# One context bank instead of two, three general banks in a ring, and new written-out orders for all engines of a cross-attention kernel

## The reference

```
qn = layer_norm(q, q_norm_g, q_norm_b);  kvn = layer_norm(kv, kv_norm_g, kv_norm_b)
Q, K, V = heads(qn @ Wq), heads(kvn @ Wk), heads(kvn @ Wv)
attn = softmax(einsum('bhqd,bhkd->bhqk', Q, K) / sqrt(32))
ctx = einsum('bhqk,bhkd->bhqd', attn, V)
out = q + gelu(ctx @ Wo + bo, approximate=False)
```

## Time and profile before

| what | value |
| --- | --- |
| median of 3 runs | 3454.32 us |
| the profiled execution, its time | 3452.61 us |
| its span, first to last instruction | 3450.8 us |
| TensorE clock granted, mean | 0.995 |
| PE busy | 3348.2 us, 97% |
| DVE, ACT, POOL busy | 2265.5, 2335.3, 2311.7 us: 66%, 68%, 67% |
| one batch in the middle, by the starts of its matmuls | 105.46 us |

### The profile page before, as it was taken

One profiled execution on the slowest core, in us unless ns is written; L12 is line 12 of the kernel. 1 busy time (PEld: TensorE's weight loads), 2 busy tenths in 40 slices (PEclk: granted clock), 3 DMA queues, 4 the chain that ended last, 5 costly groups with the idle time before them and its releaser, 6 DMA issues.

```text
span 3450.8 us, 60367 instructions
## 1 busy us (share of the span) xinstructions
PE 3348.2 (97%) x16611; PEld 2141.9 (62%) x16611; DVE 2265.5 (66%) x4775; ACT 2335.3 (68%) x3986; POOL 2311.7 (67%) x1543
## 2 busy tenths in 40 slices
PE   7999999999999999999999999999999999999998
PEld 5566666666666666666666666666666666666664
DVE  6666666676676666666766766666667667666664
ACT  4576666766666766667666667666676666676665
POOL 1767666767667676677676676766776766767665
PEclk9999999999999999999999999999999999999999
DMA  5556566556556565665565565656655655656553
GB/s 131 78 103 101 97 107 106 82 103 103 105 94 95 102 101 97 107 106 82 102 103 105 94 95 102 101 97 107 107 82 101 104 105 94 95 102 101 96 83 68
DMA packets 186492, 340.15 MB, mean 99 GB/s; under 512 B 20561, under 2 KB 20577, under 8 KB 186466
## 3 DMA queue, kind: packets, MB, share of 16 engines
q1 hardware_dynamic: 186000, 339.03, 58.0%
q10 hardware_dynamic: 466, 0.80, 0.2%
HBM read 104.87 MB, written 33.55 MB: 40 GB/s over the span
## 4 chain that ended last, share of the span: by engine, by line
PE 79%; DVE 10%; issue 6%; ACT 5%; DMA 0%; DVEq 0%; POOL 0%; ACTq 0%
PE gen L788 36%; PE score L807 14%; PE score L814 12%; PE ctx L833 11%; DVE maxes L654 6%; PE gen L845 4%; ACT probs L517 2%; PE gen L879 1%; ACT xT L542 1%; DVE ctx_n L665 1%; DVE cT L635 1%; PE gen L899 1%; DVE gen L695 1%; ACT act_out L534 1%; ACT cT L542 1%
## 5 line engine op out<-in xcount | busy, mean ns | idle before, releaser
L436 POOL TENSOR_TENSOR probs<-probs 128x1024 f32<-128x1024 f32 x762 | 1803.8, 2398 | 342.7 <-PE ctx L833 338.3
L654 DVE TENSOR_REDUCE maxes<-score 128x1 f32<-128x512 f32 x2048 | 1313.4, 681 | 210.5 <-PE score L814 197.1
L517 ACT ACTIVATE probs<-score 128x512 f32<-128x512 f32 x2048 | 1122.0, 604 | 223.5 <-PE score L807 195.5
L814 PE MATMUL score<-k_stack,q_stack 96*128 96x512 f32 x2048 | 746.8, 427 | 5.9 <-DMA q_stack<-q_nat 3.8
L807 PE MATMUL score<-q_stack,k_stack 128*128 128x512 f32 x2048 | 734.7, 420 | 11.2 <-ACT q_stack L569 5.8
L451 POOL TENSOR_TENSOR rstd<-var_eps,minus_half 128x1 f32<-128x1 f32 x256 | 141.6, 553 | 639.1 <-DVE neg_mean L685 638.8
L807 PEld LDWEIGHTS score<-q_stack,k_stack 128*128 128x128 f32 x2048 | 375.8, 188 | 254.1 <-ACT probs L517 118.7
L814 PEld LDWEIGHTS score<-k_stack,q_stack 96*128 96x128 f32 x2048 | 376.0, 188 | 246.4 <-ACT probs L517 72.9
L833 PE MATMUL ctx<-probs,v_sb 128*32 128x512 f32 x4096 | 480.5, 598 | 0.0
L788 PE MATMUL gen<-w_v,cT 128*128 128x512 f32 x1536 | 413.7, 394 | 0.6 <-issue 0.6
L788 PE MATMUL gen<-xT,w_q 128*128 128x512 f32 x1536 | 396.9, 394 | 6.7 <-ACT v_sb L528 6.6
(11 more groups left out here) (92 smaller groups left out, 2801.6 us busy)
## 6 DMA issues: line engine op xcount, KB each, us to landing
k_stack<-k_nat SPq DMA_DIRECT2D x384, 256.0 KB, 6.7
q_stack<-q_nat SPq DMA_DIRECT2D x381, 256.0 KB, 6.8
tok<-in_x SPq DMA_DIRECT2D x132, 256.0 KB, 10.4
tok<-in_ctx SPq DMA_DIRECT2D x128, 256.0 KB, 10.8
res<-in_x SPq DMA_DIRECT2D x124, 256.0 KB, 2.8
out<-res SPq DMA_DIRECT2D x124, 256.0 KB, 2.9
probs<-in_L_xattn_Wq SPq DMA_DIRECT2D x1, 1024.0 KB, 8.5
probs<-in_L_xattn_Wk SPq DMA_DIRECT2D x1, 1024.0 KB, 10.7
```

What stands on the lines that cost most here:

```text
L436: pool.tensor_tensor(probs[:, c + 1, heads], probs[:, c + 1, heads], probs[:, c, heads], ALU.add).then_inc(pool_added, 1)
L517: act.activation(probs[:, n, part, :], score_at(s, "st", i)[:], ACT.Exp, scale=SCALE).then_inc(exp_done, 1)
L654: dve.tensor_reduce(maxes[:, u1 % 2, SROW + i:SROW + i + 1], score_at(s, "s", i)[:], AX_X, ALU.max, negate=True).then_inc(max_done, 1)
L814: pe.matmul(score_bank(pe, b, s, "s", i)[:, :], q_stack[0:KROWS, u1 % 2, n, P * part:P * (part + 1)], k_stack[0:KROWS, u1 % 2, n, :], star ...
```

## The change

The context bank becomes one, and the general banks three, taken in turn by position in the list of a batch (`bank_before` gives the tile that had the bank last, across the batch boundary too). The wait of the first `pv` half of unit t is now for `cn` of unit t - 1. The orders of all five engines are written anew: the same items, 200 of TensorE's for each batch in both versions, in other places. In the list of TensorE the two halves of `pv` now stand apart in all four steps (before: in steps 1 and 3), and `z` stands apart from `pv` in all (before: in all but step 3). At the end of the last batch and in the preparation some products use other banks.

```diff
...
 
 
 PARTS = 3
+NGEN = 3
+NSCORE = 4
 OVER_BATCH = ("v", "o", "gelu", "res_add", "store", "res", "load", "ln", "la", "lv", "norm", "x", "first_res", "ob")
 ORDER = {
     "pe": (
-        "q*3 z st*4 v*2 st*2 s v s*2 st*2 v s st*2 s v s st s*2 v st s st s st s st s st s*4 pv*2 m k*3 o*3",
-        "st*2 q st*2 q st q st k*2 st*2 k x st*2 s st pv s*3 z st x s st*2 s x st x st s*3 x pv x*2 s*4 x o*4 s o "
-        "s*2 o m o*2",
-        "o k st*2 k s*2 k st*2 s st z st*2 s st s st s st s st s st s st s st*2 s st s*5 pv*2 m q*3",
-        "k*2 st*3 k q st*2 q st*3 q st*4 pv z s st*4 s*2 v s pv s*4 v s*2 v s*3 v s*2 v s v m",
+        "q*2 v q st*4 v st s v s st s st v st*2 s*2 z st v st s st v s*3 st pv s st s*2 k st s st s*3 pv m o k*2 "
+        "o",
+        "st*3 o st*3 q*3 st z st x st x st k st k*2 s st s x st x st*3 pv x s*2 x s*2 pv s*2 x s*2 o*2 s o x s*4 "
+        "o*2 s o*2 m",
+        "o*2 k*2 s st s st k st z st s st s st s st*2 s st*2 s*2 st s st q st*4 pv s*4 q s*2 q s pv m",
+        "k q v k st*4 k st*2 q st*4 q st z st*4 v st s*3 pv s*4 v s*3 v s*2 v s*3 v s pv m",
     ),
     "act": (
-        "q st*6 split st*2 v st*3 norm st*5 v mh mx*3 k mx norm*2",
-        "st*2 gelu st*2 q st*4 x norm st k st norm st norm st x st*2 x st*2 x norm x norm x*3 gelu*2 mh mx*4 "
-        "split",
-        "gelu st*2 k st*14 split mh mx*3 q mx",
-        "st*8 k st*4 q st*4 v split v mh mx*4",
+        "q st*12 v norm split norm v st*4 norm mh mx*4 k",
+        "st*6 gelu q st x*2 st*3 norm st norm st x k norm x st*4 x norm x norm x gelu x mh gelu mx*4 split",
+        "gelu st k st*11 split st*4 q mh mx*4",
+        "st*6 k st*5 q st*5 v split v mh mx*4",
     ),
     "dve": (
-        "q zt zr zb cn ln s ln s*2 ln la*2 s lv s la s*3 lv s*4 ln la s lv s*2 lv s md ml k ln",
-        "ln ob la ln q la lv ln s lv x la lv k la s*3 zt s x lv s x s*2 zr x*2 s zb x*2 s cn x s*2 ob s*4 ob md "
-        "ml ob",
-        "s*2 k s zt s zr s*9 zb s*2 cn s md ml q",
-        "k s q zt zr s*2 zb cn s*13 md ml",
+        "q s ln s*2 ln*2 la s*2 la lv zt la zr lv zb s cn lv s*10 md ml ln k",
+        "ob ln*2 la*2 ln la lv ln q lv zt zr la x*2 lv zb la cn s lv s x lv k x s*2 x s x s*3 x s*3 ob s*4 x s md "
+        "ob ml",
+        "ob s*2 zt s*2 zr s zb s*4 cn k s*7 md q ml",
+        "k zt zr zb cn q s*16 md ml",
     ),
     "pool": (
-        "ln*2 split ln add*5 res_add ln*2 add",
-        "ln*3 add*4 res_add*2 add split add",
-        "res_add add*6 split",
-        "add*5 split add",
+        "ln*3 split add*6",
+        "ln*2 res_add ln*2 add ln add*3 res_add add res_add add split",
+        "split add*6",
+        "res_add add split add*5",
     ),
     "sp": (
-        "load*7 rq load rk store res",
-        "rk rq store res store*2",
-        "first_res rk rq",
+        "load*8 rq rk",
+        "store res rq rk store res store",
+        "rk first_res rq store",
         "first_res rq rk",
     ),
 }
...
             _off = _s + {"q": 2, "k": 2, "m": 1, "z": -1}[_kind]
             GEN_AT[(_kind, _off % NU)] = len(GEN)
             GEN.append((_kind, _off // NU, _off % NU, NU))
-assert len(GEN) % 2 == 0
+
+
+def bank_before(i, count, banks):
+
+    batch, at = divmod(i, count)
+    return i - banks if at >= banks else batch * count - 1 - (count - 1 - at) % banks
 
 
 def build(nc, x, ctx_in, q_g, q_b, kv_g, kv_b, wq, wk, wv, wo, bo, out):
...
-        score = [ps(f"score{i}") for i in range(NC)]
-        ctx_ps = [ps(f"ctx{i}") for i in range(2)]
-        gen = [ps(f"gen{i}") for i in range(2)]
+        score = [ps(f"score{i}") for i in range(NSCORE)]
+        ctx_ps = ps("ctx")
+        gen = [ps(f"gen{i}") for i in range(NGEN)]

...
-                return (ctx_ps[NU % 2], gen[1 - GEN_AT[("z", NU - 1)] % 2])[n]
+                return gen[(GEN_AT[("z", NU - 1)] + 1 + n) % NGEN]

...
             return b + (s + off) // NU, (s + off) % NU
 
         def gen_at(kind, n):
-            return gen[GEN_AT[(kind, n)] % 2]
+            return gen[GEN_AT[(kind, n)] % NGEN]
 
         def gen_bank(eng, b, kind, n):
 
-            back = GEN_AT[(kind, n)] - 2
+            back = bank_before(GEN_AT[(kind, n)], len(GEN), NGEN)
             while back > -3 * len(GEN):
                 kind2, off, n2, per = GEN[back % len(GEN)]
                 b2 = b + off + back // len(GEN)
                 if valid(b2):
                     wait(eng, free[kind2], b2 * per + n2 + 1)
                     break
-                back -= 2
+                back = bank_before(back, len(GEN), NGEN)
             return gen_at(kind, n)
 
         def score_at(s, kind, i):
-            return score[SCORE_AT[(s, kind, i)] % NC]
+            return score[(PER_STEP * s + SCORE_AT[(s, kind, i)]) % NSCORE]
 
         def score_bank(eng, b, s, kind, i):
-            back = PER_STEP * s + SCORE_AT[(s, kind, i)] - NC
+            back = bank_before(PER_STEP * s + SCORE_AT[(s, kind, i)], PER_STEP * NU, NSCORE)
             while back > -2 * PER_STEP * NU:
                 b2, s2 = b + back // (PER_STEP * NU), back % (PER_STEP * NU) // PER_STEP
                 kind2, i2 = SCORES[s2][back % PER_STEP]
...
                         if kind == "cn" and valid(bp):
                             wait(dve, z_spread, tp + 1)
                             wait(dve, pv_done, 4 * tp + 4)
-                            dve.tensor_tensor(ctx_n[:], ctx_ps[up % 2][:], ctx_n[:], ALU.mult).then_inc(ctx_read, 1)
+                            dve.tensor_tensor(ctx_n[:], ctx_ps[:], ctx_n[:], ALU.mult).then_inc(ctx_read, 1)
                         if kind == "ln" and valid(b + 1):
                             wait(dve, tile_loaded[n], 16 * (b + 2))
                             dve.bn_stats(stats[:, n, :], tok[:, n, :]).then_inc(ln_stats, 1)
...
                             pe.matmul(score_bank(pe, b, s, "s", i)[:, :], q_stack[0:KROWS, u1 % 2, n, P * part:P * (part + 1)],
                                       k_stack[0:KROWS, u1 % 2, n, :], start=True, stop=True).then_inc(s_full, 1)
                         if (kind, n) == ("pv", 1) and last(b) and s == NU - 1:
-                            wait(pe, ctx_read, NU * B - 1)
                             wait(pe, ctx_split, NU * B - 2)
-                            last_products((0,), (0, 1))
                             for kind2, count in (("z", NU * B - 1), ("m", NU * B), ("q", NU * B), ("k", NU * B),
                                                  ("x", 2 * NC * B), ("v", NC * B), ("o", NC * (B - 1))):
                                 wait(pe, free[kind2], count)
-                            last_products((1,), (0, 1))
+                            last_products((0, 1), (0, 1))
                         if kind == "pv" and valid(b):
                             wait(pe, exp_done, 16 * t + 8 * n + 8)
                             if n == 0:
-                                wait(pe, ctx_read, t - 1)
+                                wait(pe, ctx_read, t)
                             if s == 0:
                                 wait(pe, free["v"], 4 * b + 2 * n + 2)
                             for c in (2 * n, 2 * n + 1):
                                 for j in range(HU):
                                     lo = P * s + DH * j
-                                    mm = pe.matmul(ctx_ps[s % 2][DH * j:DH * (j + 1), :], v_sb[:, c, lo:lo + DH],
+                                    mm = pe.matmul(ctx_ps[DH * j:DH * (j + 1), :], v_sb[:, c, lo:lo + DH],
                                                    probs[:, c, j, :], start=(c == 0), stop=(c == NC - 1))
                                     if n == AFTER_ST[s] and c % 2 == 0 and j == 0:
                                         mm.then_inc(stack_used, 1)
...
```

More of the change, by code:

```diff
@@ L314, in score_bank @@
                     break
-                back -= NC
+                back = bank_before(back, PER_STEP * NU, NSCORE)
             return score_at(s, kind, i)
@@ L617, in prepare @@
                     dve.wait_ge(bias_mm, 3)
-                    dve.tensor_copy(bias_v[:], ctx_ps[1][:, 0:NU]).then_inc(bias_cols, 1)
+                    dve.tensor_copy(bias_v[:], score[3][:, 0:NU]).then_inc(bias_cols, 1)
                     dve.wait_ge(bias_cols, 2)
@@ L627, in prepare @@
                     dve.wait_ge(bo_mm, 1)
-                    dve.tensor_copy(bias_all[:], ctx_ps[0][:]).then_inc(bo_ready, 1)
+                    dve.tensor_copy(bias_all[:], ctx_ps[:]).then_inc(bo_ready, 1)
                     low_weights(3, "o", None)
@@ L747, in prepare @@
                         for c in range(NC):
-                            mm = pe.matmul(ctx_ps[1][:, u:u + 1], probs[:, 2, c, P * u:P * (u + 1)],
+                            mm = pe.matmul(score[3][:, u:u + 1], probs[:, 2, c, P * u:P * (u + 1)],
                                            norm_cols[:, 3, c:c + 1], start=(c == 0), stop=(c == NC - 1))
@@ L762, in prepare @@
                     for u in range(NU):
```

(4 more changed lines are left out.)

## The result

The changed kernel takes 3350.9 us, the median of four runs (3350.2 to 3351.1), against 3455.1 us for the kernel before in the same series: ratio 0.9698, 95% interval 0.9682 to 0.9715. The forecast was 3376 us, faster, range 3335 to 3445. The gain is 104 us where 78 were forecast.

The account below looks back on a forecast made before the run. TensorE was taken to bound the kernel, by gaps between its starts. Per batch -1.8 (runs), -2.2 (m), +1.0 (blocks), +0.3 and +0.2 (new waits) gave -2.5 us; x 31 = -78 us, so 3376 us, range 3335 to 3445.

Parts of the forecast that it names:

- m: TensorE's waits around m in steps 1 and 3 mostly go, with more work ahead of m: -2.2 us per batch.
- Blocks: Separate groups of pv or z matmuls, twelve instead of nine, cost TensorE 0.33 us each: +1.0 us per batch.
- Runs: Scores fifth or later in an unbroken run wait for bank readers, 0.10 us each; 18 fewer: -1.8 us per batch.
- new waits: TensorE waits for cn with the single context bank, +0.3 us per batch, and for GpSimd's adds, +0.2.
- The sign for this term: Weight loads of scores waiting for exps were to fall by a third or more.
- What I had left unnamed before: Loss in a batch of the kernel before that the three named losses don't explain: 2.7 us in the prediction.
- The ends: Preparation and tail: a few tenths of a us once; the two end batches raise the count from 30 to 31.
- Rival A: Other waits, at VectorE's and ScalarE's pace, take most of the gain: -0.4 us per batch, 3442 us; chance 0.20.
- Rival B: Single context bank makes adds, z, cn and next pv a serial loop: +1.0 us per batch, 3485 us; chance 0.10.

Follow-up runs that it names:

- the edit of step 2: Changed kernel with step 2's first pv half moved beside the second, behind the step's last scores: 3549.6 us, ratio 1.0272 to the kernel before.

## Why the prediction was right, and where its sizes were off

The bound, TensorE's own starts and not its busy share, was right: a batch lost 3.1 us, the work on all engines stayed.

- *m*: forecast -2.2, measured 2.43 to 0.2. Right. The reason given for the 1.17 us of step 1 was ob alone; by the earlier trace rows ob was half of it, and the second third ahead of m did more than the move of ob.
- *Blocks*: forecast +1.0. Each lone pv half and z still costs 0.33 us in the trace after, twelve times; the edit of step 2 shows the same price. Right. The prediction's 0.44 us for an x has such a price in it too: the x itself takes 0.36 in the mean of the changed kernel, and the score behind it 0.09 more than its free pitch.
- *Runs*: forecast -1.8, and *new waits*, forecast +0.5, together -1.3. Measured is what the -3.1 of a batch leave without m and blocks: -3.1 + 2.2 - 1.0 = -1.9. The term that was mis-sized is the new waits. In the whole trace pv waits for cn once (1.1 us) and z for the adds once (0.8 us), where 0.3 and 0.2 in every batch were charged. The runs came out as forecast where they were counted: by the lateness of each score's start against the free pitches and the prices of blocks and x, the scores that stand fifth or later lose 3.2 us at 32 places before and 1.6 at 14 after, 0.10 and 0.11 each, so -1.7. But the first four scores of the runs, which had no term, lose 2.0 instead of 1.2, and what was lost in step 1 beside m is 1.2 less. What I had left unnamed before, 2.6 us, is 2.5 after. The sign for this term was badly chosen: the weight loads wait longer for exps while the counted scores lose less, so that wait doesn't measure what a run loses.
- *By place this came out otherwise.* The sums of the steps over free pitch (from the starts of matmuls, mean of 30 batches, us) and what blocks at 0.33, m, and scores at 0.10 explain of them:

| step | over, before | named | over, after | named |
| --- | --- | --- | --- | --- |
| 0 | 1.75 | 1.6 | 1.72 | 1.2 |
| 1 | 3.90 | 2.5 | 1.27 | 1.0 |
| 2 | 3.11 | 2.7 | 3.14 | 2.2 |
| 3 | 2.47 | 1.9 | 2.00 | 1.2 |

  Step 1 lost 1.2 us of unnamed waits (single scores 0.3 us late among the x); steps 0, 2 and 3 together got 1.1 that were not there, half of it step 2's late ScalarE. The right sum hides that two errors of that size cancelled. That step 2 would gain by its shorter run did not come true as long as ScalarE's read of k stood in it.
- *The ends*: a few tenths were forecast beside one more batch. The windows of the preparation are these, of the kernel before and of the changed one:

```profile
0.00:172.37 172.37, 146.82 (x656) 93.78 (x656) 106.60 (x244) 92.97 (x158) 79.71 (x76) 0.93 0.57 105
```
```profile
0.00:167.49 167.49, 146.32 (x657) 92.84 (x657) 106.55 (x244) 91.97 (x158) 72.70 (x73) 0.95 0.59 108
```

  4.9 us here and 3.7 at the tail (114.7 to 111.0) are 8.6, where x 31 had allowed 2.5. The granted clock is higher in the mean in both ends (0.93 to 0.95, 0.94 to 0.97): fewer us at half clock. As an estimate, if TensorE set the pace there, the lost clock is (1 - clock) x window: 12.1 and 6.9 us before, 8.4 and 3.3 after. So up to some 7 of the 8.6 us can be the clock, which the prediction had no term for; what of it is the order wasn't tried. 30 x 3.1 + 8.6 = 101.7 us is the difference of the two profiled spans. The medians differ by 104, since that of the kernel before lies 2.5 us above its profiled execution.

Rival A held in one place, step 2: there ScalarE's work inside the run paces TensorE until the read of k is out of it; then the pitch is the 0.33 of four banks. Rival B didn't come, neither as a wait for cn nor for the adds. But its loop is real: with a first half 4 us later it costs 3.2 us of wait, and in 22 of 30 batches the halved clock behind it.

What the orders alone, or the banks alone, are worth stays open: with two general banks the new order can't run, since TensorE would wait at z for a bank that ScalarE frees only behind exps of scores that stand after z; with one context bank the old order can't, since it has pv ahead of z in two steps. It wasn't tried with a third order.

## What to carry to other kernels

Read a saturated engine by the distances between its starts, count what it would take alone, and give each excess a place; here that gave the time within 1%, though not each place. Don't count banks or covers alone: an item inside a run of producer and consumer costs its full time if the consumer has to do it within the run, and nothing behind the run (14 us here for one word of an order moved). A written-out order that is balanced on several engines has local slacks of tenths of a us. Of the eight edits here that moved one or two items, five made it slower, two changed nothing and one made it faster; look what is queued behind the moved item, on the DMA queues too.

## What the runs showed of the hardware

- One pause of TensorE of 3.2 us in a stream of matmuls brought the granted clock from 1.00 to 0.50 in 22 of 30 batches, in 13 of them for some 6 us, so a wait of 3.2 us cost 3.0 to 5.5 us, 4.5 in the mean. A pause of 1.6 us, with shorter waits behind it, did so in 5 of 30. The mean clock of the first kernel is 0.978, that of the changed one, whose window of a batch shows 1.00, 0.997.
- Matmuls of pv and z cost 0.33 us for each block beside scores or products of the other kind of operands, whether the block has 8, 16 or 32 matmuls. The four transposes of an x cost less: behind the x at 1794.78 the score takes 0.32 us instead of 0.23, as behind every x of the changed kernel, and nothing is lost ahead of it. What in the operands makes it wasn't separated.

```profile
1795.13 0.48 PE L814 MATMUL score<-k_stack,q_stack 96*128 96x512 f32 x1
1795.45 0.64 PE L807 MATMUL score<-q_stack,k_stack 128*128 128x512 f32 x2
```
